# Main attention of a two-layer transformer block: the probabilities are turned by VectorE in 32x32 squares, and the values' products run on 32 rows each

## The reference, cut to what matters

```python
q = (rmsnorm(hidden_states @ q_a_w.T, q_a_ln_w) @ q_b_w.T).reshape(b, s, H, D_Q).transpose(0, 2, 1, 3)
kv = rmsnorm(kv_lora, kv_a_ln_w) @ kv_b_w.T
...
scores = jnp.einsum('bhqd,bhkd->bhqk', qf, kf) * scale
probs = jax.nn.softmax(scores.astype(jnp.float32), axis=-1).astype(dt)
ctx = jnp.einsum('bhqk,bhkd->bhqd', probs, v)
main_out = ctx.transpose(0, 2, 1, 3).reshape(b, s, H * D_V) @ o_w.T
```

## Time and profile before

| | us |
|---|---|
| median of three runs | 1294.52 (1292.11 to 1296.56) |
| the profiled execution | 1291.33 |
| its span in the profile | 1289.5 |
| TensorE busy | 1243.0 (96%) |
| VectorE busy | 768.3 (60%) |
| ScalarE busy | 732.9 (57%) |
| GpSimd busy | 533.4 (41%) |

### The profile page before, as it was taken

The page is one execution under the profiler, slowest core; times in us unless marked ns, Lnnn a source line. Parts: engine busy times, 40 slices in busy tenths (PEclk is TensorE's granted clock), DMA queues, the critical chain, the costliest instruction groups (busy, mean ns, idle before and its releaser), DMA issues.

```text
span 1289.5 us, 22502 instructions
## 1 busy us (share of the span) xinstructions
PE 1243.0 (96%) x8298; PEld 875.0 (68%) x8298; DVE 768.3 (60%) x1254; ACT 732.9 (57%) x1370; POOL 533.4 (41%) x531
## 2 busy tenths in 40 slices
PE   8999999999999999999999998999998998999997
PEld 5544334477777777777777777889753444678997
DVE  4689978245454444445454666555667763855555
ACT  3479978855555555555555635332355676435553
POOL 5266274248576666767666124443100000512211
PEclk9999999999999999999999999999999999989999
DMA  7780000001101011111111021020233310101111
GB/s 287 200 180 2 2 19 11 10 18 29 38 22 38 22 38 27 32 32 32 29 36 54 25 72 76 27 72 12 74 74 88 72 38 1 34 17 33 50 42 34
DMA packets 40887, 64.44 MB, mean 50 GB/s; under 512 B 8221, under 2 KB 27421, under 8 KB 39837
## 3 DMA queue, kind: packets, MB, share of 16 engines
q1 hardware_dynamic: 40776, 62.99, 17.8%
HBM read 45.60 MB, written 8.45 MB: 42 GB/s over the span
## 4 chain that ended last, share of the span: by engine, by line
PE 85%; DVE 8%; ACT 3%; issue 2%; DMA 1%; POOL 1%; SPq 0%; ACTq 0%; DVEq 0%; POOLq 0%
PE bank L1951 9%; PE bank L1883 9%; PE bank L1513 8%; PE bank L2151 6%; PE bank L2152 6%; PE bank L2153 6%; PE bank L1604 5%; PE bank L1850 5%; PE bank L1852 5%; PE bank L1851 5%; PE bank L1470 4%; PE bank L1333 3%; PE bank L1974 2%; PE bank L1450 2%; DVE mpc L1412 2%
## 5 line engine op out<-in xcount | busy, mean ns | idle before, releaser
L1859 DVE TENSOR_REDUCE nmq<-bank 128x1 f32<-128x1024 f32 x128 | 155.8, 1217 | 151.8 <-PE bank L1852 151.8
L1491 ACT ACTIVATE Pb<-bank 128x512 f32<-128x512 f32 (+3 forms) x355 | 180.6, 573 | 30.2 <-PE bank L1470 9.3
L1896 ACT ACTIVATE Pt<-bank 128x512 f32<-128x512 f32 x187 | 110.7, 594 | 118.8 <-PE bank L1883 117.9
L1874 ACT ACTIVATE Pq<-bank,nmq 128x1024 f32<-128x1024 f32 x127 | 141.7, 1116 | 58.7 <-DVE nmq L1859 58.7
L1341 DVE TENSOR_REDUCE mp<-bank 128x2 f32<-128x1024 f32 x128 | 153.5, 1221 | 27.5 <-PE bank L1333 26.7
L1883 PE MATMUL bank<-idf,Pq 128*128 128x128 f32 x1016 | 145.7, 275 | 1.4 <-ACT Pq7l L1874 1.2
L1883 PEld LDWEIGHTS bank<-idf,Pq 128*128 128x128 f32 x1016 | 119.1, 140 | 36.5 <-issue 11.9
L1412 DVE TENSOR_REDUCE mpc<-bank 128x2 f32<-128x1024 f32 (+2 forms) x96 | 88.4, 953 | 46.3 <-PE bank L1400 23.2
L1951 PE MATMUL bank<-Pt,kvx 128*64 128x256 f32 x992 | 114.1, 382 | 0.0
L1850 PE MATMUL bank<-qk1h,qk0h 128*128 128x512 f32 x256 | 109.4, 427 | 0.4 <-ACT Pq L1874 0.4
L1513 PE MATMUL bank<-Pb,vx 128*17 128x256 f32 (+3 forms) x1222 | 106.3, 407 | 0.7 <-ACT OTa L1527 0.5
(11 more groups left out here) (374 smaller groups left out, 2951.7 us busy)
## 6 DMA issues: line engine op xcount, KB each, us to landing
t<-t SPq DMA_DIRECT2D x128, 64.0 KB, 2.0
wr<-wf SPq DMA_DIRECT2D x25, 256.0 KB, 2.6
wraw<-wf SPq DMA_DIRECT2D x8, 768.0 KB, 4.6
scratch<-stgr SPq DMA_DIRECT2D x4, 1024.0 KB, 4.0
Rs<-shares SPq DMA_DIRECT2D x64, 64.0 KB, 2.7
scratch<-stg SPq DMA_DIRECT2D x8, 384.0 KB, 2.6
qst<-scratch SPq DMA_DIRECT2D x9, 256.0 KB, 8.4
owT<-owT SPq DMA_DIRECT2D x1, 2048.0 KB, 11.2
```

The source lines that it names most:

```text
L1491: e.activation(PBR[l][i % len(PBR[l])][:, 0:c], bank[b][:, 0:c], ACT.Exp, scale=0.25).then_inc(exp_ok[0], 1)
L1859: e.tensor_reduce(nmq[:, n % 8:n % 8 + 1], scores(u, i), AX, ALU.max, negate=True).then_inc(mp_ok, 1)
L1874: e.activation(probabilities(u, i)[:], scores(u, i), ACT.Exp, bias=nmq[:, n % 8:n % 8 + 1], accum_out=sums[:, u % 2, i:i + 1]).then_inc(ex ...
```

## The change

- `pe_transposed`, `act_copy` and `dve_copy` go. In their place VectorE turns each block of probabilities once, in 32x32 squares, with one `transpose` of 128x1024 from SBUF to SBUF (`dve_turn`): the square of query group `g` (partitions 32g to 32g+31) and key group `b` (32 keys) stays where it is and is transposed in itself. `PT` then holds, for each `b`, 128 columns: both heads' and both halves' 32 queries of the group `g` whose partitions they stand in.
- The values' products (`pe_pvm`) take 32 rows, 64 weight columns and 128 streaming columns each: for each of 32 key groups `b`, four products, one for each group `g`, with rows 32g to 32g+31, each into a bank of its own (4 to 7), all in partitions 0 to 63. That is 128 matmuls for a unit where 16 stood. They come in two pieces of 64, after score block 2 and after score block 3 of the next unit.
- The values are needed in each group of 32 partitions: `kv4`, loaded by sixteen DMAs (`sp_values`) once the first attention has ended.
- ScalarE moves the second head's result from partitions 0 to 63 to 64 to 127, within the banks (`act_lift`), before VectorE weighs it.
- The probabilities have three buffers in place of eight, and an exponential waits for the turn three blocks before. The projection always uses bank 7, the preparations banks 5 and 6, and all of them wait for the weighing before them.
- The order is new (`main_order`). The preparations stand after score blocks 0 and 1: at positions 0, 1, 4, 8, 9, 12 of each 16, where the unit within the group of four is the position over 4 and the remainder the block (for the first prepared pair 4, 5, 8, 9, 12, 13).
- Some entries of `BESIDE_LAST` move: the layer norm's statistics to (31, 0), its scaling to (31, 1), its transposes and the router's products behind unit 31's scores.

```diff
+    for u in range(1, 32):
+        order.append(("score", u, 0))
+        output(u - 2)
+        prep(4 * u)
+        order.extend([("rec", u - 1), ("vturn", u - 1, 3), ("expo", u, 0)])
+        order.extend(BESIDE_LAST.get((u, 0), ()))
+        order.append(("score", u, 1))
+        prep(4 * u + 1)
+        order.extend([("spread", u - 1), ("vturn", u, 0), ("expo", u, 1)])
+        order.extend(BESIDE_LAST.get((u, 1), ()))
+        order.extend([("score", u, 2), ("pv", u - 1, 0), ("vturn", u, 1), ("expo", u, 2)])
+        order.extend([("score", u, 3), ("pv", u - 1, 1), ("lift", u - 1), ("ot", u - 1), ("expo", u, 3), ("vturn", u, 2)])
+    output(30)
+    order.extend([("rec", 31), ("vturn", 31, 3), ("turn", 0), ("spread", 31), ("pv", 31, 0), ("pv", 31, 1), ("hT", 0),
+                  ("wup", 1), ("wdown", 1), ("lift", 31), ("ot", 31), ("project", 31), ("logits", 0), ("add", 31)])
...
-        if n >= 8:
-            e.wait_ge(tr_mm, 8 * (u - 2) + 8)
+        if n >= 3:
+            e.wait_ge(pt_ok, n - 2)
...
+    def dve_turn(e, u, i):
+
+        c, n = 64 * (i % 2) + 32 * (i // 2), 4 * u + i
+        e.wait_ge(exp_ok[1], n + 1)
+        if i == 0 and u >= 2:
+            e.wait_ge(pv_mm[1], u - 1)
...
+        source = probabilities(u, i)[:].rearrange("p (b k) -> p b k", k=32)
+        if u < 31:
+            e.transpose(PT[u % 2][:, :, c:c + 32], source).then_inc(pt_ok, 1)
...
-        for k in range(NT):
-            for hd in range(2):
-                last = e.matmul(bank[6][64 * hd:64 * hd + 64, 0:256], kvx[:, k, :],
-                                transposed(u, k)[:, 256 * hd:256 * hd + 256],
-                                start=(k < 1), stop=(k == NT - 1), skip_group_check=True)
-        last.then_inc(pv_mm[1], 1)
+    def pe_pvm(e, u, part):
+
+        if part == 0:
+            if u:
+                e.wait_ge(ot_ok[1], u)
+                e.wait_ge(add_ok, u)
...
+            e.wait_ge(*COPIED[u])
+            e.wait_ge(pt_ok, 4 * u + 4)
+        for b in range(16 * part, 16 * part + 16):
+            for g in range(4):
+                rows = slice(32 * g, 32 * g + 32)
+                last = e.matmul(rest[0:64, g, 0:128], kv4[b % 4][rows, b // 4, :], transposed(u, b)[rows, :],
+                                start=(b == 0), stop=(b == 31), skip_group_check=True)
+        if part:
+            last.then_inc(pv_mm[1], 1)
+
+    def act_lift(e, u):
+
+        e.wait_ge(pv_mm[1], u + 1)
+        e.activation(rest[64:128, :, 0:64], rest[0:64, :, 64:128], ACT.Copy).then_inc(lift_ok, 1)
...
+    def sp_values(e):
+
+        e.wait_ge(sh_mm, 16)
+        e.wait_ge(pv_mm[0], 128)
+        for s in range(4):
+            for g in range(4):
+                e.dma_start(kv4[s][32 * g:32 * g + 32, :, :], kvx[32 * s:32 * s + 32, :, :]).then_inc(d_kv, 16)
```

More of the change, by code:

```diff
@@ L74 @@
 BESIDE_LAST = {
-    (28, 7): [("temperature",), ("wup", 0), ("wdown", 0)],
-    (30, 6): [("stats", 0)],
-    (31, 2): [("normed", 0)],
-    (31, 5): [("turn", 0), ("hT", 0)],
-    (31, 7): [("wup", 1), ("wdown", 1)],
-    (31, "values"): [("logits", 0)],
+    (29, 0): [("temperature",), ("wup", 0), ("wdown", 0)],
+    (31, 0): [("stats", 0)],
+    (31, 1): [("normed", 0)],
 }
+PREP_AT = ((4, 5, 8, 9, 12, 13), (0, 1, 4, 8, 9, 12))
 def main_order():
-    order = [("expo", 0, 1), ("score", 0, 2), ("score", 0, 3), ("ctx", 0), ("ctx", 1), ("expo", 0, 2), ("cadd", 0),
-             ("ctx", 2), ("expo", 0, 3), ("cadd", 1), ("ctx", 3), ("cadd", 2), ("cadd", 3)]
@@ L92, in main_order @@
-    chunks = []
-    def turn(u, k):
-        order.extend([("t", u, k), ("copy", u, k)])
-        if chunks:
-            order.extend(chunks.pop(0))
-        order.extend(BESIDE_LAST.get((u, k), ()))
-    def score(u, i):
-        if u < 32:
-            order.append(("score", u, i))
-    def expo(u, i):
-        if u < 32:
-            order.append(("expo", u, i))
-    def output(u):
-        order.extend([("project", u), ("add", u)])
-    for u in range(32):
-        if u % 4 == 0 and u // 4 + 1 < 8:
-            for i in range(len(FIRST)):
-                chunks.extend([[("prep", u // 4 + 1, i), ("pcopy", u // 4 + 1, i)]] + [[]] * (PREP_EVERY - 1))
-        score(u + 1, 0)
-        turn(u, 0)
-        order.append(("rec", u))
-        score(u + 1, 1)
-        expo(u + 1, 0)
-        turn(u, 1)
-        if u:
-            order.extend([("pv", u - 1), ("ot", u - 1)])
-        expo(u + 1, 1)
-        turn(u, 2)
-        score(u + 1, 2)
-        turn(u, 3)
-        if u:
-            output(u - 1)
-        expo(u + 1, 2)
-        turn(u, 4)
-        order.append(("spread", u))
-        score(u + 1, 3)
-        turn(u, 5)
-        turn(u, 6)
-        expo(u + 1, 3)
-        turn(u, 7)
@@ L137, in main_order, with prep @@
-    assert not chunks
-    order.extend([("pv", 31)] + BESIDE_LAST[31, "values"] + [("ot", 31)])
-    output(31)
+    order = [("expo", 0, 1), ("score", 0, 2), ("ctx", 0), ("ctx", 1), ("vturn", 0, 0), ("expo", 0, 2), ("score", 0, 3),
+             ("cadd", 0), ("ctx", 2), ("vturn", 0, 1), ("cadd", 1), ("expo", 0, 3), ("ctx", 3), ("cadd", 2), ("vturn", 0, 2),
+             ("cadd", 3)]
+    preps = {16 * (p - 1) + at: (p, i) for p in range(1, 8) for i, at in enumerate(PREP_AT[p > 1])}
+    def prep(n):
+        if n in preps:
+            order.extend([("prep", *preps[n]), ("pcopy", *preps[n])])
@@ new lines, in output @@
+    def output(u):
+        if u >= 0:
+            order.extend([("project", u), ("add", u)])
+    for u in range(1, 32):
[10 more added lines that the diff above has]
+        order.extend([("score", u, 3), ("pv", u - 1, 1), ("lift", u - 1), ("ot", u - 1), ("expo", u, 3), ("vturn", u, 2)])
@@ L365, in program @@
     wide = [nc.alloc_psum_tensor(f"bank{2 * i}", [128, 2, 512], F32) for i in range(2)]
-    bank = [wide[i // 2][:, i % 2, :] for i in range(4)] + [nc.alloc_psum_tensor(f"bank{i}", [128, 512], F32)[:] for i in range(4, 8)]
+    rest = nc.alloc_psum_tensor("bank4", [128, 4, 512], F32)
+    bank = [wide[i // 2][:, i % 2, :] for i in range(4)] + [rest[:, i, :] for i in range(4)]
     x = sb("x", [128, NT, D], F32)
@@ L1616, in pe_prep @@
     def pe_prep(e, p, k):
-        b, free = PTB["prep", p, k]
+        b, free = PREP[p, k]
         e.wait_ge(*free)
+        e.wait_ge(pc_ok, len(FIRST) * p + k - 1)
         pe_part(e, p, FIRST[k], bank[b][:], (0, 1))
@@ L2826, in vector @@
                 dve_score(e, s[1], s[2])
-            elif s[0] == "copy":
-                dve_copy(e, s[1], s[2])
+            elif s[0] == "vturn":
+                dve_turn(e, s[1], s[2])
             elif s[0] == "rec":
@@ L2970, in scalar @@
                 act_expo(e, s[1], s[2])
-            elif s[0] == "copy":
-                act_copy(e, s[1], s[2])
             elif s[0] == "pcopy":
                 act_product(e, s[1], s[2])
+            elif s[0] == "lift":
+                act_lift(e, s[1])
             elif s[0] == "ctx":
```

117 lines of the change are left out of this document (38 added, 79 removed).

## The result

| | before | changed |
|---|---|---|
| median of four runs, us | 1293.32 (1288.22 to 1296.56) | 1343.68 (1340.22 to 1347.57) |
| profiled execution / its span | 1291.33 / 1289.5 | 1341.48 / 1339.7 |

The changed kernel takes 1.0394 times as long (95% interval 1.0346 to 1.0442): +50.4 us. Forecast were slower and 1318 us (+24 by the median, +27 by its own sum). The sign and the range (1290 to 1390) hold; the size is half of what came.

What follows compares the result with a forecast made beforehand. TensorE, busy 96% of the span, was taken to bound the kernel. TensorE's work +17.3, waits +13.2 and the stage's end -3.6 gave +26.9 us on 1291.33: 1318 us, range 1290 to 1390.

Steps and rivals of the forecast that it cites:

- Rounds: Values' products on TensorE: four row groups run fully side by side, 64 rounds of 0.109 us, 6.98 us a unit.
- The rival that took a third of a round as lost: Values' products: row groups share less than fully, a round takes 0.142 us, time 1386 us; chance 0.10.
- Visits: TensorE's passages into and out of split rows: 0.40 us each, two a unit, 0.80 us.
- The rival of free visits: Passages cost nothing because weights load while the last group streams: time 1296 us; chance 0.10.
- Sum of TensorE's own work: TensorE's removed and added work in each unit: +0.54 us, for 32 units +17.3 us.
- Turn and lift: VectorE's turn of 1024 columns takes 1.25 us; ScalarE's lift of 256 columns takes 0.35 to 0.4 us.
- Slow turns: Rival: VectorE's turns take 2.33 us, lengthening the chain by 2.2 us; time 1343 us; chance 0.08.
- Units without preparations: TensorE waits 0.6 us before score block 2; four such units add 2.4 us, each lasting 14.9 us.
- Units with a preparation behind block 0 only: ScalarE's copy stands before block 0's exponential: 0.65 us of waiting in 12 units, +7.8 us.
- Unit 31: Layer norm's statistics and scaling stand in the chain on VectorE: +3 us (between 0 and 5).
- End of the stage: From last score block to last projection: 17.2 us instead of 20.8, -3.6 us.
- Units with two preparations: A preparation behind block 1 (some 1.2 us) covers the 0.6 us wait; only +0.54 us a unit.

Runs made afterwards that it cites:

- the third visit: Eight key groups of the second values' piece moved into the middle of score block 3, against the best that keeps the whole computation: 1322.5 us, ratio 1.0227.
- the last kernels: Changed kernel with two copy buffers, third turn before lift, single preparations behind block 1: 1317.3 us; with unit 31's old order back: 1314.9 us.
- The two-buffer kernel: Changed kernel with a second SBUF buffer taking every other copy of a prepared product: 1325.3 us, ratio 1.0238.
- The best that keeps the whole computation: Changed kernel with two copy buffers, third turn before lift except in unit 31, single preparations behind block 1: 1314.9 us, ratio 1.0156.
- the turn ahead: Third turn before lift and weighing, here with two copy buffers and single preparations behind block 1, against the changed kernel: 1317.3 us, ratio 1.0168.

## Why the prediction was right in its sign and short in its size

By its own steps, against the profile of the changed kernel:

- **Rounds.** 64 rounds x 0.109 = 6.98 were forecast. A piece of 128 records lasts 3.72 us: (3.72 - 0.27)/32 = 0.108. Right: four groups of rows lie side by side without loss. The rival that took a third of a round as lost, and with it the figure of 3.07 for four row groups that the Trainium skill gives ("TensorE: Matmul & The Clock Gate", "Measured speedup vs the span model"), is not what this trace has (the Trainium skill's row there is for 512 columns, these stream 128): it has the full four.
- **Visits.** 0.40 forecast, 0.35 read in each, 0.36 by the third visit. Two make 0.70 where 0.80 stood. The rival of free visits falls. (The period of the earlier trace rows holds one float32 product of two records, not two products; its 0.86 us is right.)
- **Sum of TensorE's own work.** -7.00 - 0.32 + 0.08 + 6.98 + 0.70 = +0.44, forecast +0.54. Units without preparations show it: 13.74 + 0.44 = 14.18, and with the 0.5 us of waits that remain in the last kernels 14.69.
- **Turn and lift.** 1.224 and 0.357 us, forecast 1.25 and 0.35 to 0.4. The forecast's own terms for the turn (0.212, and 992 columns at the maxima's step) make 1.20, not 1.25; nothing hangs on it. Slow turns: no.
- **Units without preparations.** A wait of 0.6 us in front of score block 2; the profile has 0.64, and 0.81 counted from start to start. Unit 15.04, forecast 14.9.
- **Units with a preparation behind block 0 only.** 0.65 forecast; the profile has 0.39, and 0.56 counted from start to start.
- **Unit 31.** +3 forecast; the unit before the last takes 15.2 us, so next to nothing came of it.
- **End of the stage.** -3.6 forecast, 18.5 - 21.5 = -3.0.
- **Units with two preparations: the step that failed.** "A preparation (some 1.2 us) behind block 1 covers this" and "The preparations keep their products". They keep them, but not their banks: in the changed kernel they write banks 5 and 6, where the values' products follow, so those wait for the copies, and the second copy for GpSimd, which reads the first out of the only buffer for 4.0 us (712.77 to 716.8). Before, preparations and values' products had banks apart. This wait belongs to "New waits" and was not looked for; the sum had +0.54 for these units, and +2.22 came.

The sum with what was measured: 32 x 0.44 = 14.1; waits 4 x 0.81 + 12 x 0.56 = 10.0; two-preparation units 14 x (2.22 - 0.44) = 24.9; the end -3.0: 46.0 us. (The six units with twelve records wait some 0.4 us less than this has, and the fifteenth such unit, ahead of the first projection, waits 1.3 us, so the term is about 1 us high.) From the stage's first score block to its last projection the two profiles differ by 47.2 us, and the spans by 50.2; 3.0 us lie outside the stage and are left unexplained. Without the failed step the sum is 21 to 24 us, near the forecast 27, in part because the +3 for unit 31, which did not come, stood against 3 us outside the stage that nobody forecast. The two-buffer kernel, at +30.8 by its ratio, shows as much; what it has beyond that is in part the wait for `Rs`, 2 us in two units.

The prediction named the sign of its error (it is wrong "if the units with preparations wait too") and gave it no price, though the diff shows the wait on `COPIED` and the line that sets the banks.

No version here beats the kernel before. The best that keeps the whole computation is at 1.0156, and what it lacks is seen: 32 x 0.44 us of TensorE, mostly visits, 0.5 us of waits in each unit without preparations, and the wait for `Rs` in some with twelve records. The last of these no run tried to remove. Fewer visits leave VectorE without work, and more tiles run into the instruction supply.

## What to carry to other kernels

A layout that uses a quarter of TensorE's rows and runs four such tiles side by side gained nothing over whole rows here; it only pays if what it removes costs more than the passages between modes, 0.35 us each. When a change gives one PSUM bank two users, follow the other user's wait to its end, through the copy and through whoever reads the copy's destination; a single SBUF buffer, read by GpSimd, cost 20 of the 50 us here. Look at the order of a DMA queue too: what stands in front of a small read-back can hold the engine that waits for it. And count the instructions of small products: stretches that used 256 of them in 3.5 us ran on almost undisturbed, and in those that used them in 2 us or less TensorE often stood for the next.

## What the runs showed of the hardware that was not expected

- Four row groups of 32 rows run fully side by side: 128 records of 128 columns in 3.72 us, one every 27 ns.
- Eight tiles of 32 rows and 64 columns bring a record every 10.6 to 11.3 ns where nothing interrupts them, 0.085 to 0.09 us for a round in which each streams only 64 columns.
- The supply of instructions is a bound of its own: 82 gaps of 0.3 to 4.8 us (139 us in all) with 512 instructions in a piece, 23 gaps (22.9 us) with 256 in 2 us, one or two gaps with 256 in 3.5 us. Every one of the 82 and the 23 ends 1.2 to 1.6 us after an instruction packet has ended.
- With eight tiles a stretch of 3 us in which TensorE was busy for 1.20 us was followed by a granted clock of 0.50, the 1.2 GHz level, from 705 to 711. At the end of the stage, with the turn ahead, a wait of 3.28 us was followed by it from 775 to 784 (9.56 us for products that take 7.76).
- VectorE's turn of 128x1024 float32 in 32x32 squares takes 1.224 us, about as long as a maximum over as many columns (1.198).
